# Counting the last edges in tiles as well, in place of gathering their rows (graph network, two layers)

## The chip, the cores and the metric

One NeuronCore of a Trainium2 chip runs the kernel. The metric is the device time of one execution in microseconds. The engines are named as in the profile: PE (TensorE, PEld its weight loads), DVE (VectorE), ACT (ScalarE), POOL (GpSimd) and SP (SyncE, which here only issues DMAs).

## The reference

A graph of 6250 nodes with 128 features has 206,250 edges, sorted by destination `dst`. Layer 0 is a linear map with batch norm and a normalized sum over edges; layer 1 sums the 128 attributes of each edge into its destination and puts the result through three linear maps.

```python
h = jnp.maximum(_layernorm(x), 0.0)
H = h @ W.T + b                       # then batch norm over the nodes
dinv = rsqrt(1.0 + segment_sum(ones, dst))
msg = H[src] * (dinv[src] * dinv[dst])[:, None]
out = segment_sum(msg, dst) + H * (dinv * dinv)[:, None]
x = x + relu(out)
h = jnp.maximum(_layernorm(x), 0.0)
agg = segment_sum(edge_attr, dst)
z = relu(concat([h, agg, u[batch]]) @ W1 + b1)
x = x + relu(z @ W2 + b2) @ W3 + b3
```

## The kernel before, in words

The kernel runs five stages, each a block with one hand-written instruction stream per engine, tied by semaphores.

1. **Opening.** Loads, layer norm, linear map, degree counts. Besides the edge rows for the attributes it loads the last 27,648 edges' `dst` and `src` (`raw_g`) and turns them into `grel` and `index`.
2. **Plan.** The scaled features H·dinv are put into `table_sb` in SBUF as two fp16 parts, high and low, and written to the DRAM tensor `scaled_h_table`. The nodes are dealt out in groups of WN = 3. A tile holds up to 128 edges of one group. `gather_sources` reads the 128 `src` entries that start at each tile's first edge (14 indirect DMAs by POOL, one per 128 tiles) and from them come `src_lo` (source modulo 128) and `key` (source block times 3, plus which of the 3 destination nodes). Groups with more than 128 edges get spare tiles.
3. **Step loop,** S = 27 steps, the bulk of the time. On PE a step `s` has
   - *build*: TS = 68 tiles; `build_tile` multiplies `lo_hot` by `key_hot` (both compared into being by DVE, eight tiles at a time, an "oct", 9 per step, the ninth with only 4 tiles), a 128x147 table of counts, into `ps_counts`. ACT copies four tiles at a time (a "quad") into `counts_sb` (`save_quad`, 17 per step).
   - *multiply*: 98 products (49 blocks x high and low) of `table_sb` with the counts of the *previous* step, 204 columns each (68 tiles x 3 nodes), dealt out between the builds by `PART`.
   - *attributes*: `sum_attr`, 60 matmuls (120 PE passes) with `attr_hot` in three batches, whose sums are put into place by a `place` matmul with a `place_hot` and added by DVE (`add`).
   - *rows*: the last 27,648 edges are not counted but gathered: POOL issues 8 indirect DMAs per step that fetch rows of `scaled_h_table` into `gathered`, with four buffers (`rows_used` frees them, so that they run up to two steps ahead); `sum_rows` sums them with `half_hot`, 16 matmuls at q = 13 and q = 30, plus a fourth place, copy and add.
   - The edge attributes stream in beside all this, three loads of 1280 KB per step from SP.
   Step 13 is the step of the spare tiles; in steps 15 to 23 DVE adds 8 spare groups each (`add_spares`, L1436). The first three steps stand apart, the others are a PE loop of two steps per round. DVE, ACT and POOL are written out in full.
4. **Last product** of the loop (98 products with nothing to build).
5. **MLP.** Layer norm, three linear maps, output.

The order inside a step is set by hand: PE by the tile number `q` (`SUM_AT`, `ROWS_AT`, the `if q ==` lines), DVE by the oct number `b`, ACT by the quad number `k`. POOL issues its gathers in one queue, each pair of a step waiting for `rows_used`.

Of the kernel before, what the change touches and what calls it, by code (L numbers as in the profile page):

```python
# [8 lines left out]
F16 = mybir.dt.float16  # L9
# [9 lines left out]
GR = 2  # L19
GG = GR * P  # L20
# [7 lines left out]
KINDS = R + 1  # L28
WN = 3
TS = 68  # L30
# [6 lines left out]
def gnn_kernel(nc, x, src, dst, edge_attr, w_gcn, b_gcn, gamma, beta, u, w1, b1, w2, b2, w3, b3, out):  # L37
# [12 lines left out]
    KC = KINDS * S  # L50
# [8 lines left out]
    EDGES = E - GB * GG  # L59
    assert D == P and FULL == R * GB - 2 and E % GE and GB <= P and KEYS <= 256  # L60
    assert FB == NB - 1 == (CHUNKS - 1) * BC and AW >= NB * P and CC % DB == 2 * S % DB == 0 and N < NOWHERE / 2
    assert MC <= GC and MAIN * WN <= N and 0 < EDGES <= E - P and DEGS >= NB
# [5 lines left out]
    table = nc.dram_tensor("scaled_h_table", (NB * P, 2 * P), F16, kind="Internal").ap()  # L68
    src_elements = src.rearrange("(e a) -> e a", a=1)
    attr_last = edge_attr[E - GE:E, :].rearrange("(p t) f -> p (t f)", t=GT)  # L70
    x_full = x[0:FB * P, :].rearrange("(b p) f -> p b f", p=P)
    table_blocks = table.rearrange("(b p) f -> p b f", p=P)
    out_full = out[0:FB * P, :].rearrange("(b p) f -> p b f", p=P)

    with ExitStack() as ctx:
# [17 lines left out]

        dinv = sb("dinv", [P, NB])
# [3 lines left out]
        grel = sb("grel", [P, GR, GB], I16)  # L98
# [3 lines left out]
        index = sb("index", [P, GB, GR], I32)  # L102
        slot_node = sb("slot_node", [P, KINDS, S])
        slot_now = sb("slot_now", [P, KINDS, S])
        chunk_start = sb("chunk_start", [1, S, KINDS])
        starts = sb("starts", [1, S, KINDS])
        starts_int = sb("starts_int", [1, S, KINDS], I32)
# [216 lines left out]
        with ExitStack() as scope:  # L324
            raw_d = sb("raw_d", [GB, R, GE], I32, scope)
            raw_g = sb("raw_g", [GB, 2, GG], I32, scope)
            edge_f, grow, drow = (sb(n, [GB, R, GE], scope=scope) for n in ("edge_f", "grow", "drow"))
            gather_f, gather_row, src_row = (sb(n, [GB, GG], scope=scope) for n in ("gather_f", "gather_row", "src_row"))
# [3 lines left out]
            minus_lim = sb("minus_lim", [GB, KINDS], scope=scope)  # L332
# [9 lines left out]
            group_span = sb("group_span", [GB, KINDS], scope=scope)  # L342
            lim = sb("lim", [GB, 2 * KINDS + 1], scope=scope)
# [3 lines left out]
            by_slot = sb("by_slot", [GB, KINDS, CG, W], scope=scope)  # L347
# [5 lines left out]
            start_all = sb("start_all", [P, KINDS, S], scope=scope)  # L353
# [5 lines left out]
            low_rows = ps_rows_t[0:1, 0:BC, :].rearrange("a b f -> a (b f)")[:, 0:KINDS * GB]  # L359
            high_rows = ps_rows_t[0:1, BC:2 * BC, :].rearrange("a b f -> a (b f)")[:, 0:KINDS * GB]  # L360
# [5 lines left out]
            (eps_ok, counting, dst_in, gather_dst_in, src_in, w_in, zeroed, ident_ok, consts, pen_ok, src_ok, tiles_ok,  # L366
# [20 lines left out]
            with nc.Block() as block:  # L387
# [233 lines left out]
                def _(act):  # L621
# [25 lines left out]
                    for c in range(CHUNKS + 1):  # L647
# [12 lines left out]
                        if c in TURN_AT:  # L660
                            save_turn(2 * R + TURN_AT.index(c))
# [4 lines left out]
                def _(pe):  # L666
                    def turn_rows(k):
                        if 2 <= k < 2 * R:
                            pe.wait_ge(turn_read, k - 1)
                        elif k > 2 * R:  # L670
                            pe.wait_ge(turn_read, k)
# [1208 lines left out]
```

## Time and profile before

| | |
|---|---|
| median of 3 runs | 872.0 us (870.55 to 873.07) |
| profiled execution, its own time | 876.41 us |
| its span | 874.7 us |
| granted PE clock, mean | 0.93 of full speed |
| busy over the span | PE 727.7, DVE 589.4, ACT 416.2, POOL 320.2 us |
| step loop, first half_hot to last product | 138.7 to 793.1 us |

Busy times of engines overlap, so they don't add up to the span. The profiled execution is one execution. Differences worked out from its trace are applied to the median.

### The profile page before, as it was taken

Reading aid. Unit: us, or ns where it says so; the run is one execution under the profiler, and the core shown is the slowest. Engines: PE = TensorE matmul, PEld = TensorE weight load, DVE = VectorE, ACT = ScalarE, POOL = GpSimd, SP = SyncE. Lnnn points to the kernel's source line nnn. Section 1 sums busy time; section 2 is a strip of 40 time slices with the busy share of each in tenths; the row PEclk is TensorE's granted clock in tenths of the full one; section 3 lists DMA queues with packets and bytes.
Section 4 is the critical chain, followed back from the end, with each engine's and each line's share of the span. In section 5 each row is a group of like instructions: output and inputs, shape, how many; then the busy total and the mean of one; then the engine's idle time right before and its main releaser. Section 6 shows DMA issues by size and latency. Waiting matters only on the chain. (4 is left out here: it accounts for less than half of the span.)

```text
span 874.7 us, 23162 instructions
## 1 busy us (share of the span) xinstructions
PE 727.7 (83%) x9280; PEld 579.9 (66%) x9280; DVE 589.4 (67%) x1328; ACT 416.2 (48%) x810; POOL 320.2 (37%) x318
## 2 busy tenths in 40 slices
PE   1987765399898898998889888989988888998796
PEld 0756653277777776777777667777766677887464
DVE  6997955357666666776666567767776666753854
ACT  1442553344444545455445444444544454553693
POOL 3403825543334333333333444332333333003523
PEclk9986575599999999999999999999999999999899
DMA  6101732456665556655556556555655555533013
GB/s 173 25 1 38 256 97 92 120 191 205 205 197 181 172 199 202 201 184 177 184 202 204 174 175 204 185 167 188 201 181 161 201 196 175 187 94 84 0 46 103
DMA packets 78377, 136.20 MB, mean 156 GB/s; under 512 B 6706, under 2 KB 32844, under 8 KB 78328
## 3 DMA queue, kind: packets, MB, share of 16 engines
q1 hardware_dynamic: 70904, 120.50, 42.6%
q0 software_dynamic: 7424, 15.12, 5.6%
q8 instruction: 21, 0.34, 0.2%
q14 instruction: 28, 0.23, 0.1%
HBM read 129.19 MB, written 6.41 MB: 155 GB/s over the span
## 5 line engine op out<-in xcount | busy, mean ns | idle before, releaser
L1316 ACT CAST counts_sb<-ps_counts 128x588 f16<-128x588 f32 x459 | 295.1, 651 | 337.3 <-PE ps_counts L1493 239.7
L1493 PE MATMUL ps_counts<-key_hot,lo_hot 128*128 128x147 bf16 x1836 | 368.8, 237 | 77.6 <-ACT counts_sb L1316 49.6
L1501 PE MATMUL ps_product<-counts_sb,table_sb 128*128 128x204 f16 x2646 | 403.3, 252 | 1.5 <-issue 1.3
L1304 POOL DMA_INDIRECT gathered<-scaled_h_table,index x216 | 238.1, 1102 | 382.0 <-PE ps_sums L1531 306.4
L1493 PEld LDWEIGHTS ps_counts<-key_hot,lo_hot 128*128 128x128 bf16 x1836 | 181.1, 101 | 146.1 <-issue 70.7
L1359 DVE TENSOR_TENSOR lo_hot<-src_lo,iota_key 128x1024 bf16<-128x1024 f16 (+1 forms) x243 | 160.7, 661 | 171.4 <-PE ps_counts L1493 147.5
L1501 PEld LDWEIGHTS ps_product<-counts_sb,table_sb 128*128 128x128 f16 x2646 | 236.2, 98 | 5.3 <-issue 4.1
L1364 DVE TENSOR_TENSOR key_hot<-key,iota_key 128x1176 bf16<-128x1176 f16 (+1 forms) x243 | 177.7, 731 | 0.0
L1516 PE MATMUL ps_sums<-attr,attr_hot 128*32 128x128 f32 x3240 | 130.7, 285 | 0.0
L1516 PEld LDWEIGHTS ps_sums<-attr,attr_hot 128*32 128x32 f32 x3240 | 85.4, 112 | 27.9 <-issue 19.2
L1375 DVE TENSOR_TENSOR attr_hot<-rel,iota_w 128x640 f32<-128x640 int16 x81 | 66.6, 823 | 29.1 <-remote 21.4
L1540 PE MATMUL ps_product<-place_hot,sums_sb 128*128 128x96 f32 x216 | 44.0, 286 | 0.0
L1540 PEld LDWEIGHTS ps_product<-place_hot,sums_sb 128*128 128x128 f32 x216 | 33.8, 197 | 1.8
L1419 DVE TENSOR_TENSOR acc<-acc,ps_product 128x96 f32 x108 | 26.9, 249 | 4.3 <-PE ps_product L1540 4.1
L1667 POOL TENSOR_TENSOR x_ring<-attr,b_rows 128x512 f32<-128x512 f32 (+1 forms) x13 | 15.7, 1211 | 30.7 <-DVE y_ring L1743 30.4
L1392 DVE TENSOR_SCALAR place_hot<-iota_c,slot_now 128x96 f32<-128x96 f32 x108 | 26.3, 265 | 0.0
L1531 PE MATMUL ps_sums<-gathered,half_hot 128*32 128x128 f16 x432 | 19.2, 223 | 5.4 <-issue 3.9
L1759 ACT ACTIVATE relu_ring<-ps_t,dinv 128x128 f32<-128x128 f32 x49 | 14.0, 370 | 20.4 <-PE ps_t L1807 20.0
L1653 POOL MEMSET attr<- 128x128 f32 x1 | 0.2, 205 | 59.8 <-POOLq L1277 59.8
L1326 ACT COPY sums_sb<-ps_sums 128x128 f32<-128x128 f32 x81 | 22.0, 272 | 0.0
L985 ACT ACTIVATE table_sb<-ps_rows,dinv 128x128 f16<-128x128 f32 x49 | 14.0, 381 | 15.0 <-PE ps_rows L908 14.0
L1775 ACT ACTIVATE h_ring<-attr,shift,rstd 128x128 f32<-128x128 f32 x49 | 20.1, 486 | 0.8 <-DVE shift L1701 0.8
(291 smaller groups left out, 667.6 us busy)
## 6 DMA issues: line engine op xcount, KB each, us to landing
attr<-in_edge_attr_dram SPq DMA_DIRECT2D x80, 1280.0 KB
gathered<-scaled_h_table,index POOLq DMA_INDIRECT x216
acc<-in_x_dram SPq DMA_DIRECT2D x4, 768.0 KB, 8.5
scaled_h_table<-table_sb SPq DMA_DIRECT2D x12, 256.0 KB
attr<-in_x_dram SPq DMA_DIRECT2D x12, 256.0 KB, 5.1
out_dram<-y_ring SPq DMA_DIRECT2D x12, 256.0 KB, 2.4
attr<-in_edge_attr_dram SPq DMA_DIRECT2D x2, 320.0 KB, 3.2
attr<-in_edge_attr_dram SPq DMA_DIRECT2D x1, 640.0 KB
```

The costliest lines, as they stand in the source:

```text
L1304: pool.indirect_dma_start(gathered[:, n % GATHERS, g, :], None, table, bass.IndirectOffsetOnAxis(ap=index[:, s * CG + g, t:t + 1], axis=0) ...
L1316: act.copy(counts_sb[s % 2][:].rearrange("p h (n t) -> p h n t", n=WN) [:, :, :, k * QUAD:(k + 1) * QUAD], ps_counts[n % 2][:, :, 0:KEYS]. ...
L1326: act.copy(sums_sb[:, 1, :], ps_sums[:, 1, 0:P]).then_inc(sums_saved, 1)
L1359: v.tensor_tensor(lo_hot[:, n % 2, 0:pairs], src_lo[:, tiles].rearrange("p (b c) -> p b c", c=2).unsqueeze(2) .to_broadcast(whole), iota_l ...
L1364: v.tensor_tensor(key_hot[:, n % 2, 0:pairs], key[:, tiles].rearrange("p (b c) -> p b c", c=2).unsqueeze(2) .to_broadcast(whole), iota_key ...
L1375: v.tensor_tensor(attr_hot[:, a % 2], rel[:, r, :, s * CG:(s + 1) * CG].unsqueeze(3) .to_broadcast(whole), iota_w[:].unsqueeze(1).unsqueez ...
L1392: v.tensor_scalar(place_hot[:, n % 2, :], iota_c[:], slot_now[:, kind, s:s + 1], None, ALU.is_equal).then_inc(place_hots, 1)
L1419: v.tensor_tensor(win, win, new, ALU.add).then_inc(added, 1)
L1493: ins = pe.matmul(ps_counts[(odd + quad) % 2][:, c, 0:KEYS], lo_hot[:, held, pair, :, q % 2], key_hot[:, held, pair, :, q % 2], start=True ...
L1501: ins = pe.matmul(ps_product[side][:, 0:SLOTS], table_sb[:, h, low, :], counts_sb[side][:, h, :], start=(part == 0), stop=(part == 2 * NB ...
L1516: ins = pe.matmul(ps_sums[g * W:(g + 1) * W, 1, 0:P], attr_hot[:, held, t, g, :], attr[:, j * CG + g, t * P:(t + 1) * P], start=(t == 0), ...
L1540: pe.matmul(ps_product[side][:, WIN + window * WC:WIN + (window + 1) * WC], sums_sb[:, which, :], place_hot[:, parity, :], start=True, sto ...
```

## The change

The last edges are counted in tiles like all others. TS goes from 68 to 80 tiles per step, so 26 x 80 tiles of 3 nodes cover 6240 of the 6250 nodes, and the rest fall to the spare tiles. The gathering of rows goes, with everything that served it: the `raw_g` loads, `grel`, `index`, their two turns on PE and ACT, the fourth of each KINDS table, the table in DRAM and its 13 writes, the 216 gather DMAs, `half_hot`, `sum_rows`, `save_rows`, one of the four places and adds per step. Each step's products get 240 columns in place of 204, and the octs are all full (10 per step), the quads 20. A tile now may begin within 128 edges of the end of `src`, so the source reads go to `src_padded`, a DRAM copy with 128 more entries, copied by SP in the opening; POOL waits for it ahead of its first source gather. There are 17 source gathers in place of 14, and a fifth batch of keys. The place hots are made by POOL, which has nothing else to do in the loop, and no longer by DVE.

```diff
-TS = 68
+TS = 80
...
+                    sp.dma_start(src_padded[0:E].rearrange("(a f) -> a f", f=SRC_ROW),
+                                 src.rearrange("(a f) -> a f", f=SRC_ROW)).then_inc(src_copied, 16)
...
-                    for c in range(CHUNKS):
-                        n = width(c)
-                        sp.wait_ge(low_ready, c + 1)
-                        sp.dma_start(table_blocks[:, c * BC:c * BC + n, :],
-                                     table_sb[:, c * BC:c * BC + n, :, :].rearrange("p b a f -> p b (a f)"))\
-                          .then_inc(table_out, 16)
...
-        OCTS = -(-TS // OCT)
+        OCTS = TS // OCT
...
-        SUM_AT = {q: (j, tiles) for j, places in enumerate(((5, 13), (26, 34), (47, 56)))
+        SUM_AT = {q: (j, tiles) for j, places in enumerate(((6, 15), (32, 41), (58, 67)))
                   for q, tiles in zip(places, (range(0, 3), range(3, GT)))}
-        ROWS_AT = {13: 0, 30: 1}
...
-                            pool.wait_ge(table_out, 16 * CHUNKS)
-                            for s in range(S):
-                                for t in range(GR):
-                                    n = s * GR + t
-                                    if n >= GATHERS:
-                                        pool.wait_ge(rows_used, n - GATHERS + 1)
-                                    for g in range(CG):
-                                        pool.indirect_dma_start(
-                                            gathered[:, n % GATHERS, g, :], None, table,
-                                            bass.IndirectOffsetOnAxis(ap=index[:, s * CG + g, t:t + 1], axis=0),
-                                        ).then_inc(gather_in[n % GATHERS], 16)
+                            for n in range(PLACES):
+                                s, kind = divmod(n, R)
+                                if n >= 2:
+                                    pool.wait_ge(placed, n - 1)
+                                pool.tensor_scalar(place_hot[:, n % 2, :], iota_c[:], slot_now[:, kind, s:s + 1], None,
+                                                   ALU.is_equal).then_inc(place_hots, 1)
...
-                                    if q in ROWS_AT:
-                                        sum_rows(s, odd, loads, ROWS_AT[q], first)
-                                    if q == 6 and not first:
+                                    if q == 7 and not first:
                                         pe.wait_ge(sums_saved, s * R)
-                                        place(s * 4 - 2, 0, 1, side, 0)
-                                    if q == 16 and not first:
-                                        pe.wait_ge(rows_saved, s)
-                                        place(s * 4 - 1, 1, 0, side, 1)
-                                    if q == 24:
+                                        place(s * 3 - 1, (odd + 1) % 2, side, 0)
+                                    if q == 28:
                                         pe.wait_ge(sums_saved, s * R + 1)
-                                        place(s * 4, 0, 1, side, 2, first)
-                                    if q == 42:
+                                        place(s * 3, odd, side, 1, first)
+                                    if q == 52:
                                         pe.wait_ge(sums_saved, s * R + 2)
-                                        place(s * 4 + 1, 1, 1, side, 0)
+                                        place(s * 3 + 1, (odd + 1) % 2, side, 0)
```

What moves on PE in the step loop, at tile q = 13 of a step before, where the second part of the first attribute batch and the first half of the gathered rows stand (`L1493` is a build, `L1501` a product, `L1516` the attributes, `L1531` the rows, `L1540` a place):

```order
L1501 MATMUL ps_product<-counts_sb,table_sb 128x204 x2
L1516 MATMUL ps_sums<-attr,attr_hot 32x128 x8
L1531 MATMUL ps_sums<-gathered,half_hot 32x128 x8
L1493 MATMUL ps_counts<-key_hot,lo_hot 128x147
L1501 MATMUL ps_product<-counts_sb,table_sb 128x204
```

and at the same part of a step after (`L1397` is the build, `L1405` the product, `L1420` the attributes):

```order
L1405 MATMUL ps_product<-counts_sb,table_sb 128x240
L1420 MATMUL ps_sums<-attr,attr_hot 32x128 x8
L1397 MATMUL ps_counts<-key_hot,lo_hot 128x147
L1405 MATMUL ps_product<-counts_sb,table_sb 128x240
L1397 MATMUL ps_counts<-key_hot,lo_hot 128x147
L1405 MATMUL ps_product<-counts_sb,table_sb 128x240 x2
```

The rows are gone, each product is 36 columns wider, and fewer products stand between two builds (98 dealt over 80 tiles).

DVE at the turn from one step to the next, before (`L1359` and `L1364` make an oct, `L1375` is `attr_hot`, `L1392` the place hots, `L1384` `half_hot`, `L1419` an add):

```order
L1419 TENSOR_TENSOR acc<-acc,ps_product 128x96
L1359 TENSOR_TENSOR lo_hot<-src_lo,iota_key 128x512
L1364 TENSOR_TENSOR key_hot<-key,iota_key 128x588
L1359 TENSOR_TENSOR lo_hot<-src_lo,iota_key 128x1024
L1364 TENSOR_TENSOR key_hot<-key,iota_key 128x1176
L1392 TENSOR_SCALAR place_hot<-iota_c,slot_now 128x96 x2
L1384 TENSOR_TENSOR half_hot<-grel,iota_w 128x256
L1359 TENSOR_TENSOR lo_hot<-src_lo,iota_key 128x1024
```

and after, from the last add of a step on (`L1296` and `L1301` make an oct, `L1340` is an add, `L1312` the `attr_hot`):

```order
L1340 TENSOR_TENSOR acc<-acc,ps_product 128x96
L1296 TENSOR_TENSOR lo_hot<-src_lo,iota_key 128x1024
L1301 TENSOR_TENSOR key_hot<-key,iota_key 128x1176
L1296 TENSOR_TENSOR lo_hot<-src_lo,iota_key 128x1024
L1301 TENSOR_TENSOR key_hot<-key,iota_key 128x1176
L1296 TENSOR_TENSOR lo_hot<-src_lo,iota_key 128x1024
L1301 TENSOR_TENSOR key_hot<-key,iota_key 128x1176
L1312 TENSOR_TENSOR attr_hot<-rel,iota_w 128x640
```

The half oct at a step's end is a full one, and the three small compares behind the step's first oct are gone from DVE. POOL's whole part in the loop was

```order
L1295 UNCONDITIONAL_BRANCH
L1304 DMA gathered<-scaled_h_table,index 128x256 x216
L1277 UNCONDITIONAL_BRANCH
L1243 REGISTER_ALU
L1243 COMPARE_AND_BRANCH
```

and is now

```order
L1246 UNCONDITIONAL_BRANCH
L1252 TENSOR_SCALAR place_hot<-iota_c,slot_now 128x96 x81
L1228 UNCONDITIONAL_BRANCH
L1194 REGISTER_ALU
L1194 COMPARE_AND_BRANCH
```

so that it issues no DMA there at all.

## Rows read from the trace of the kernel before

**Rows 1.** Windows: us; busy (x) PE, PEld, DVE, ACT, POOL; PEclk; DMA share; GB/s.

```profile
138.73:173.94 35.21, 18.13 (x207) 11.95 (x206) 15.20 (x30) 10.98 (x21) 24.42 (x23) 0.60 0.41 123
173.94:743.40 569.46, 505.88 (x7437) 409.46 (x7436) 390.24 (x813) 278.14 (x505) 212.50 (x192) 0.98 0.57 189
502.33:719.98 217.65, 189.72 (x2793) 154.09 (x2791) 151.99 (x348) 104.32 (x189) 80.96 (x72) 0.98 0.56 185
743.40:763.79 20.39, 19.91 (x313) 16.65 (x311) 15.85 (x33) 11.67 (x21) 0.00 (x0) 1.00 0.58 200
763.79:784.00 20.21, 20.21 (x318) 17.18 (x315) 13.78 (x29) 11.67 (x21) 0.00 (x0) 1.00 0.17 56
```

**Rows 2.** The half_hot of each step on DVE (one tile's instructions).

```profile
L1384 DVE TENSOR_TENSOR half_hot<-grel,iota_w x27: 417/419/423, 138.7 to 763.8; 128x256 f16<-128x256 int16 x27
```

**Rows 3.** Timeline of two steps around their gathers: start us, length us, idle before in brackets.

```profile
395.30 1.20 ACT L1316 CAST counts_sb<-ps_counts 128x588 f16<-128x588 f32 x2 [3.12 <-remote]
...
421.15 0.82 DVE L1375 TENSOR_TENSOR attr_hot<-rel,iota_w 128x640 f32<-128x640 int16 x1 [1.97 <-remote]
421.19 0.65 ACT L1316 CAST counts_sb<-ps_counts 128x588 f16<-128x588 f32 x1 [2.73 <-PE ps_counts L1493]
...
421.97 0.24 PE L1493 MATMUL ps_counts<-key_hot,lo_hot 128*128 128x147 bf16 x1 [1.84 <-ACT counts_sb L1316]
```

**Rows 4.** Timeline of PE in step 25: builds, products, rows, a place.

```profile
745.43 0.38 PE L1540 MATMUL ps_product<-place_hot,sums_sb 128*128 128x96 f32 x2
745.65 0.23 PE L1493 MATMUL ps_counts<-key_hot,lo_hot 128*128 128x147 bf16 x1
745.72 0.25 PE L1501 MATMUL ps_product<-counts_sb,table_sb 128*128 128x204 f16 x1
745.81 0.23 PE L1493 MATMUL ps_counts<-key_hot,lo_hot 128*128 128x147 bf16 x1
...
747.58 0.29 PE L1531 MATMUL ps_sums<-gathered,half_hot 128*32 128x128 f16 x8
747.81 0.24 PE L1493 MATMUL ps_counts<-key_hot,lo_hot 128*128 128x147 bf16 x1
...
763.57 0.24 PE L1493 MATMUL ps_counts<-key_hot,lo_hot 128*128 128x147 bf16 x1 [0.48 <-DVE key_hot L1364]
```

**Rows 5.** Timeline of step 0: the long waits.

```profile
163.60 1.38 ACT L1316 CAST counts_sb<-ps_counts 128x588 f16<-128x588 f32 x2 [5.70 <-remote]
...
172.23 1.20 ACT L1316 CAST counts_sb<-ps_counts 128x588 f16<-128x588 f32 x2 [7.25 <-remote]
```

**Rows 6.** Timeline of ACT: copies of quads in the plain part of a step.

```profile
387.21 1.45 ACT L1316 CAST counts_sb<-ps_counts 128x588 f16<-128x588 f32 x2 [1.03 <-PE ps_counts L1493]
```

**Rows 7.** Timeline of the opening: POOL compares, a DVE operation under a POOL memset, edge work.

```profile
28.28 0.53 POOL L462 TENSOR_SCALAR ident_part<-ident 128x128 f16<-128x128 f32 x1
...
68.71 3.66 DVE L183 TENSOR_SCALAR unscale<-ident,size 128x128 f32<-128x128 f32 x1
...
66.90 5.39 POOL L482 MEMSET acc<- 128x6346 f32 x1 [34.60 <-DVE h_ring L556]
...
17.15 0.28 DVE L506 CAST gather_f<-raw_g 108x256 f32<-108x256 int32 x1
...
18.46 0.16 DVE L510 TENSOR_REDUCE lim<-tile_min 108x3 f32<-108x15 f32 x1
```

**Rows 8.** Groups by line, the plan's costs: us busy, mean ns.

```profile
L1064 DVE TENSOR_TENSOR passed<-count_row,sizes 128x1792 f16<-128x1792 f16 x3 | 3.6, 1195 | 0.0
```

**Rows 9.** Timeline of the plan's end: source gathers, the stall, the last two key batches.

```profile
114.83 1.13 POOL L225 DMA_INDIRECT spare_raw<-in_src_dram,spare_int  x1 [0.30 <-issue]
115.90 0.59 ACT L992 COPY acc<-ps_self 128x512 f32<-128x512 f32 x1 [4.28 <-remote]
...
130.89 0.59 ACT L1004 CAST key<-ps_keys 128x512 f16<-128x512 f32 x1 [1.38 <-PE ps_keys L934]
...
133.60 0.35 ACT L1004 CAST key<-ps_keys 128x232 f16<-128x232 f32 x1 [1.34 <-PE ps_keys L934]
```

More of the change, by code:

```diff
@@ L442, in _ @@
                     pool.wait_ge(lims, 1)
-                    for r in range(KINDS):
+                    for r in range(R):
                         whole = [GB, CG, W]
@@ L687, in _ @@
                     pe.wait_ge(lims, 1)
-                    for k in range(2 * KINDS + 1):
-                        if k < KINDS:
+                    for k in range(2 * R + 1):
+                        if k < R:
                             row = low_rows[:, k * GB:(k + 1) * GB]
-                        elif k < 2 * KINDS:
-                            row = high_rows[:, (k - KINDS) * GB:(k - KINDS + 1) * GB]
+                        elif k < 2 * R:
+                            row = high_rows[:, (k - R) * GB:(k - R + 1) * GB]
                         else:
@@ L706, in find_slots @@
                         pe.wait_ge(consts, CONSTS)
-                        for r in range(KINDS):
+                        for r in range(R):
                             of_slot = by_slot[:, r].rearrange("g c n -> g (c n)")
@@ L1192, in _ @@
                         def _(sp):
-                            for s in (summed, rows_used, last_in, x_loaded, *attr_in):
+                            for s in (summed, last_in, x_loaded, *attr_in):
                                 sp.sem_clear(s)
@@ L1347, in _ @@
                         def _(v):
-                            regs = [[v.alloc_register(f"start{k}_{j}") for j in range(KINDS)] for k in range(2)]
+                            regs = [[v.alloc_register(f"start{k}_{j}") for j in range(R)] for k in range(2)]
                             base_regs = [v.alloc_register(f"base{j}") for j in range(SPARE_ADDS)]
@@ L1520, in sum_attr, with place @@
                                     ins.then_inc(summed, 1)
-                            def sum_rows(s, odd, loads, t, first):
-                                if t == 0:
-                                    pe.wait_ge(rows_hots, s + 1)
-                                    if not first:
-                                        pe.wait_ge(rows_saved, s)
-                                held = odd * GR + t
-                                pe.wait_ge(gather_in[held], loads)
-                                for part in range(2):
-                                    for g in range(CG):
-                                        ins = pe.matmul(ps_sums[g * W:(g + 1) * W, 0, 0:P], half_hot[:, t, g, :],
-                                                        gathered[:, held, g, part * P:(part + 1) * P],
-                                                        start=(t == 0 and part == 0), stop=(t == GR - 1 and part == 1))
-                                ins.then_inc(rows_used, 1)
-                            def place(n, parity, which, side, window, first=False):
+                            def place(n, parity, side, window, first=False):
                                 pe.wait_ge(place_hots, n + 1)
```

249 lines of the change are left out of this document (81 added, 168 removed).

## The prediction

> **What bounds the kernel now.** I first cut the loop into steps, at the half_hot that DVE makes once in each [rows 2], and asked for the busy time in windows between them [rows 1]. Steps 1 to 24 take 569.46 us, 23.73 each, with PE busy 505.88 of it, DVE 390.24, ACT 278.14. PE is the engine that sets the pace, but it is idle 63.6 us, 2.6 per step. The next two windows show what that idle time is. POOL's gathers run up to two steps ahead, so that the last two steps, 25 and 26, have none (POOL 0.00). They take 20.39 and 20.21 us, with PE busy for 19.91 and 20.21. Step 25 has its other work whole, and its DMA traffic is even a little higher (200 GB/s against 189), so bandwidth isn't what the other steps lack.
>
> The timeline shows what a step with gathers suffers. Once in each, while POOL is issuing, all engines that wait for PE stand still together: at 421.15 and 421.19 DVE and ACT come out of waits of 1.97 and 2.73 us at the same moment, and PE, having run ahead, then waits 1.84 us for ACT; a step earlier ACT waited 3.12 us [rows 3]. The profile calls the releaser "remote", that is, it found none. In step 0, where POOL issues 23 of them in one series [rows 1], the same waits are 5.70 and 7.25 us [rows 5], and in the plan, at the end of the series of source gathers, 4.28 us [rows 9]. I don't know the mechanism. What I rely on is that the waits stand where POOL issues indirect DMAs, and that two steps without them have none.
>
> **The change, term by term** (as a difference; the profiled execution took 876.41 us, its span 874.7, the median is 872.0, and I take the same difference for each).
>
> *Stall removed.* If all 24 steps ran like step 25 they would save 24 x (23.73 - 20.39) = 80.1 us. Not all of the excess is the gathers'. The nine steps with spare adds average 24.18 (217.65 / 9), the other fifteen (569.46 - 217.65) / 15 = 23.45; the 0.73 of difference, 6.6 us in sum, is DVE's and stays. Some 1.2 us I leave for the first product step, in which PE's clock is still rising. That leaves **-72.3 us**.
>
> *PE's added work per step.* In the clean step a product takes 0.09 us from start to start, a build 0.07, a group of rows 0.23 (747.58 to 747.81), a place 0.22 [rows 4]. A product of 240 columns scales to 0.087 x 240/204, which is 0.015 more (0.087 is an estimate over several pairs of these rows); 98 of them +1.50. Twelve builds at 0.073: +0.88. Three more quad boundaries, about +0.1. Two groups of rows: -0.46, one place: -0.22. At the start of the step PE waits 0.48 for DVE, because the half oct covers only four tiles while DVE makes the next; with full octs I take off half of it, -0.24. Sum +1.56, so a clean step is 20.39 + 1.6 = 22.0. Bounds: 21.6 if the wait goes whole and a boundary costs nothing; 22.9 if another pacer comes in (below). Over steps 1 to 26: 26 x 1.6 = **+41.6 us**.
>
> *Who hides the rest.* DVE makes 10 octs for 8.5; even if its whole 15.85 us grew with them it would be busy 18.6 of 22.0 us, and it loses half_hot, the place hots and one add: still hidden. ACT goes from 17 to 20 quads of 0.65: 11.67 becomes at most 13.6. Two quads in a row take ACT 1.45 and one takes 0.65, so they follow one another at 0.80 [rows 3, 6]. PE's four builds and their share of products take about 0.80 both before (4 x 0.073 + 5.8 x 0.087) and after (4 x 0.073 + 4.9 x 0.102), so ACT is no closer to the path than it was, but it has no slack. The edge loads have 22 us for what now passes in 20.4.
>
> *Step 0* takes 35.21 us at a clock of 0.60. Its two long waits are 12.95 us; waits of PE for gathered rows are another 1.4 (an estimate, between nothing and the 7.25 of its longest wait). What is left, 20.9 us for 8.5 octs, is 2.3 per oct without its first; 1.5 octs more cost 3.4. Sum **-10.9 us**. If these waits had another cause it would be +3.4.
>
> *Last product.* 98 x 0.015 = **+1.5 us**.
>
> *Plan.* The three compares (3.6 us together [rows 8]) grow by 17/14: +0.8. The spare compares, for which no row stands here, grow by 80/68; bounded by the same 3.6 us group and nothing, I take +0.8. At the end, batches of keys follow one another at 2.7 us (130.89 to 133.60) [rows 9], each waiting on the one before: the fourth batch has four columns in place of two and there is a fifth of one column: +2.4, between +1.6 and +5.4. Three more source gathers are three more POOL instructions of some 1.13 us [rows 9], behind which only the last batches' data wait; 0, or up to +4 if the stall of 4.28 us there grows with the series. Writing the table to DRAM goes and may shorten that stall; the two I let cancel. Sum **+4.0 us**.
>
> *Opening.* DVE is rid of the four operations between 17.15 and 18.46 [rows 7], in a run without idle time: -1.3, and of smaller tables: **-1.4 us**. The copy of `src` is issued by SP behind the loads of x, and the first to need it is the plan's first source gather, behind the whole opening (its row at 68.71 is still ahead of that) [rows 7].
>
> *Spare adds* now take ten steps, not nine: **+0.7 us**.
>
> Sum: -72.3 + 41.6 - 10.9 + 1.5 + 4.0 - 1.4 + 0.7 = -36.8. From 872.0 that gives **835 us**.
>
> **A rule that speaks against the change.** While POOL's memset of 5.39 us ran, a DVE compare-sized operation on 128x128 took 3.66 us, where POOL itself needs 0.53 for one of that size, and it ended with the memset [rows 7]: the two engines can hold each other up. The place hots put 81 POOL operations of about 0.53 us (by the compare of 128x128 [rows 7]) beside DVE's compares. The Trainium skill states it as a rule (SBUF — State Buffer, "Who interferes with whom"): a DVE instruction with two SBUF inputs contends with a GpSimd instruction that reads SBUF, and whoever comes second waits in full. By that rule DVE could lose 3 x 0.53 = 1.6 us per step. The trace agrees on a blocking as such; how much of it reaches PE it can't show. From the rows alone: DVE has at least 3.4 us idle per step (22.0 less 18.6), in which 1.6 us fit, so I price it at 0, with the whole 1.6 as the worst.
>
> **The rivals.**
> - *Another pacer, 11 in 100.* The stall goes, but the step comes out at 22.8, because ACT's quads (no slack, above) or DVE's late octs hold PE: 26 x 0.8 = +21, and half of step 0's long waits stay, +6: 862. For it: the 0.80 on both sides. Against: step 25 shows PE 19.91 busy of 20.39 with the same ratio.
> - *Everything a little better, 13 in 100.* A clean step is 21.6 (-10), the spare adds hide in it now that DVE isn't thrown back by the stall (-7), the plan's stall is gone (-3): 815.
> - *Slower, 5 in 100.* The place hots on POOL hold up DVE, and through the octs PE. They sit between the octs, three per step. To eat the whole gain the step must lose 36.8 / 26 = 1.4 us more, 0.47 us per place hot, of the 0.53 that one lasts: nearly each would have to be passed on in full. With the 1.6 of the worst case and the other terms at their high bounds the time is about 885. Against it stands DVE's idle time.
> - *The change doesn't do what it says, 1 in 100.* If there were more spare tiles than 80 the whole loop would run twice, some 600 us more. Groups of three nodes have 99 edges on average, so few pass 128.
> - The forecast as it stands: 70 in 100, its own range 822 to 850.
>
> **How the numbers follow.** The likeliest case gives 835. The range reaches down to the better case and up towards the other pacer: 815 to 858. A difference of 0.3% (2.6 us) is about what a measurement of this kernel can tell from none. Faster gets the forecast, the better case and the other pacer: 0.94; slower 0.05; the same 0.01, since nothing but a chance sum of mishaps ends there.
>
> **What would show it.** Steps of 21.6 to 22.3 us in the windows, all alike but for the spare steps, with PE at least 97% busy and the granted clock at 1.00 throughout (0.98 over the gathered steps [rows 1]). No wait of ACT of 2 us or more with the releaser "remote" inside steps. Step 0 near 24 us. DVE 16 to 18 us per step; POOL about 1.6 us. Products 15 ns longer. The plan's end some 4 us later relative to its start. Wrong I would be if the waits of 2 to 3 us are still there without the gathers (then they belong to code loading or the like, and the time is near 905), if PE shows short waits for ACT at each quad, or if DVE's compares grow longer beside POOL.

## The result, and the profile after

Beside each other on one chip the kernel before takes 872.35 us and the changed one **811.63 us** (ratio 0.929, 95% interval 0.926 to 0.931): 60.7 us less, where I had forecast 37. The direction is right, the size is not, and the time lies 3 us below my range. The experiments then added what this pair doesn't show: in three of the five later sets of runs the same kernel before took 781 to 783 us, and in the one of them in which the changed kernel ran too, it was the slower, at 803.9.

First the page of the changed kernel: busy time, then PE, POOL and PE's clock in 40 slices.

```profile
span 807.7 us, 22520 instructions
PE 724.6 (90%) x9123; PEld 589.2 (73%) x9123; DVE 611.8 (76%) x1230; ACT 464.8 (58%) x864; POOL 203.6 (25%) x184
PE   1876565899999999999999999999999999999797
POOL 3402880222222112222211221222221121204424
PEclk9997755899999999999999999999999999999899
```

PE stays at 9 from the first product step to the end of the loop. Now both traces, cut at the same marks: start of the plan, first lo_hot of the loop (step 0), first lo_hot of step 1, first lo_hot of step 25, last product taken, end. These are the prediction's own stretches: step 0 by itself, then steps 1 to 24. Windows (columns as in [rows 1]), first of before:

```profile
83.33:136.70 53.37, 33.62 (x274) 29.97 (x274) 34.75 (x109) 25.56 (x75) 27.51 (x29) 0.63 0.51 160
136.70:172.29 35.59, 17.93 (x204) 12.02 (x204) 15.58 (x27) 9.37 (x18) 25.64 (x24) 0.60 0.39 120
172.29:741.75 569.46, 505.52 (x7429) 409.07 (x7430) 390.24 (x812) 278.29 (x506) 212.50 (x192) 0.98 0.57 188
741.75:793.12 51.37, 50.38 (x739) 43.61 (x738) 32.07 (x66) 24.80 (x45) 0.00 (x0) 1.00 0.51 160
793.12:874.70 81.58, 65.42 (x325) 43.95 (x325) 46.61 (x119) 50.77 (x126) 31.52 (x27) 0.92 0.15 42
```

and of the changed kernel, with eleven of its plain steps in the last row:

```profile
81.57:143.54 61.97, 36.75 (x289) 30.99 (x289) 37.58 (x111) 26.89 (x78) 33.34 (x33) 0.61 0.28 90
143.54:160.68 17.14, 13.32 (x199) 9.26 (x200) 16.57 (x27) 10.68 (x20) 5.30 (x4) 0.86 0.47 156
160.68:677.26 516.58, 507.88 (x7283) 423.15 (x7281) 409.43 (x727) 321.42 (x553) 103.85 (x72) 1.00 0.55 183
677.26:731.98 54.72, 54.68 (x732) 46.93 (x730) 33.05 (x55) 28.81 (x50) 7.30 (x5) 1.00 0.51 154
731.98:807.70 75.72, 63.95 (x325) 42.76 (x325) 46.65 (x119) 50.53 (x126) 31.48 (x27) 0.95 0.15 44
207.63:440.40 232.77, 232.76 (x3347) 194.79 (x3345) 182.65 (x299) 147.38 (x254) 48.36 (x34) 1.00 0.56 186
```

| piece | forecast | measured |
|---|---|---|
| start to plan | -1.4 | 81.57 - 83.33 = -1.76 |
| plan | +4.0 | 61.97 - 53.37 = +8.60 |
| step 0 | -10.9 | 17.14 - 35.59 = -18.45 |
| steps 1 to 24 | -72.3 + 24 x 1.6 + 0.7 = -33.2 | 516.58 - 569.46 = -52.88 |
| steps 25 and 26, last product | 2 x 1.6 + 1.5 = +4.7 | 54.72 - 51.37 = +3.35 |
| behind the loop | 0 | 75.72 - 81.58 = -5.86 |
| sum | -36.8 | -67.0 |

The spans differ by 67.0, the medians by 60.7: the profiled execution of before was 4.1 us above its median, that of after 1.9 below.

A plain step is 232.77 / 11 = 21.16 us with no idle time of PE, not 22.0. The steps with spares are longer. One of them on DVE (start, length), then the instruction of PE that waits for what follows the additions:

```profile
469.81 2.29 DVE L1352 TENSOR_TENSOR acc<-acc,spare_sums 128x3 f32 x8
472.01 0.69 DVE L1296 TENSOR_TENSOR lo_hot<-src_lo,iota_key 128x1024 bf16<-128x1024 f16 x1
472.62 0.76 DVE L1301 TENSOR_TENSOR key_hot<-key,iota_key 128x1176 bf16<-128x1176 f16 x1
473.44 0.24 PE L1397 MATMUL ps_counts<-key_hot,lo_hot 128*128 128x147 bf16 x1 [0.74 <-DVE key_hot L1301]
```

The eight additions take 2.29 us in a row, the oct behind them is late, and PE waits 0.74 us, once in each such step. In the plan, while POOL issues its series of source gathers, ACT still has the waits that nothing in the profile releases, the only ones left in the kernel:

```profile
117.33 0.59 ACT L954 COPY acc<-ps_self 128x512 f32<-128x512 f32 x1 [2.88 <-remote]
120.86 1.14 ACT L947 ACTIVATE table_sb<-ps_rows,dinv 128x128 f16<-128x128 f32 x4 [2.94 <-remote]
123.05 0.59 ACT L954 COPY acc<-ps_self 128x512 f32<-128x512 f32 x1 [1.05 <-remote]
```

### The profile page after: what moved, and what is told of

It is laid out like the page before. It is cut to its first block and busy times, and to the rows that moved or that the text cites. A ratio compares the mean times of both kernels' runs of the same rounds, so it can differ in the third digit from the quotient of the medians.

```text
span 807.7 us, 22520 instructions
## 1 busy us (share of the span) xinstructions
PE 724.6 (90%) x9123; PEld 589.2 (73%) x9123; DVE 611.8 (76%) x1230; ACT 464.8 (58%) x864; POOL 203.6 (25%) x184
## 5 line engine op out<-in xcount | busy, mean ns | idle before, releaser
L1262 ACT CAST counts_sb<-ps_counts 128x588 f16<-128x588 f32 x540 | 350.6, 651 | 219.8 <-PE ps_counts L1397 186.4
L1405 PE MATMUL ps_product<-counts_sb,table_sb 128*128 128x240 f16 x2646 | 442.4, 264 | 0.0
L1397 PE MATMUL ps_counts<-key_hot,lo_hot 128*128 128x147 bf16 x2160 | 410.5, 231 | 14.5 <-DVE key_hot L1301 11.7
L1296 DVE TENSOR_TENSOR lo_hot<-src_lo,iota_key 128x1024 bf16<-128x1024 f16 x270 | 186.3, 690 | 107.8 <-PE ps_counts L1397 103.4
L1397 PEld LDWEIGHTS ps_counts<-key_hot,lo_hot 128*128 128x128 bf16 x2160 | 206.7, 98 | 74.0 <-issue 43.7
L1405 PEld LDWEIGHTS ps_product<-counts_sb,table_sb 128*128 128x128 f16 x2646 | 243.5, 97 | 10.6 <-issue 0.2
L1252 POOL TENSOR_SCALAR place_hot<-iota_c,slot_now 128x96 f32<-128x96 f32 x81 | 116.6, 1439 | 471.8 <-PE ps_product L1430 449.4
L1301 DVE TENSOR_TENSOR key_hot<-key,iota_key 128x1176 bf16<-128x1176 f16 x270 | 208.8, 774 | 0.0
L1420 PE MATMUL ps_sums<-attr,attr_hot 128*32 128x128 f32 x3240 | 122.7, 279 | 0.0
L1420 PEld LDWEIGHTS ps_sums<-attr,attr_hot 128*32 128x32 f32 x3240 | 79.0, 109 | 26.0 <-issue 24.9
L1312 DVE TENSOR_TENSOR attr_hot<-rel,iota_w 128x640 f32<-128x640 int16 x81 | 66.9, 826 | 0.0
L1430 PE MATMUL ps_product<-place_hot,sums_sb 128*128 128x96 f32 x162 | 30.3, 269 | 0.0
L1052 DVE SCALAR_TENSOR_TENSOR table_sb<-ps_rows,dinv,table_sb 128x128 f16<-128x128 f32 x49 | 13.7, 340 | 9.1 <-issue 7.6
L849 POOL DMA_INDIRECT src_raw<-src_padded,begin_int x17 | 19.0, 1116 | 4.1 <-issue 4.1
```

The lines of the kernel that those rows point to most:

```text
L849: pool.indirect_dma_start(src_raw[:, k, :], None, src_elements, bass.IndirectOffsetOnAxis(ap=begin_int[:, k:k + 1], axis=0))\
L1252: pool.tensor_scalar(place_hot[:, n % 2, :], iota_c[:], slot_now[:, kind, s:s + 1], None, ALU.is_equal).then_inc(place_hots, 1)
L1262: act.copy(counts_sb[s % 2][:].rearrange("p h (n t) -> p h n t", n=WN) [:, :, :, k * QUAD:(k + 1) * QUAD], ps_counts[n % 2][:, :, 0:KEYS]. ...
L1296: v.tensor_tensor(lo_hot[:, n % 2], src_lo[:, tiles].rearrange("p (b c) -> p b c", c=2).unsqueeze(2) .to_broadcast(whole), iota_lo[:].unsq ...
L1301: v.tensor_tensor(key_hot[:, n % 2], key[:, tiles].rearrange("p (b c) -> p b c", c=2).unsqueeze(2) .to_broadcast(whole), iota_key[:].unsqu ...
L1312: v.tensor_tensor(attr_hot[:, a % 2], rel[:, r, :, s * CG:(s + 1) * CG].unsqueeze(3) .to_broadcast(whole), iota_w[:].unsqueeze(1).unsqueez ...
```

## The experiments

Behind the first pair, which is at the upper level, five sets of runs followed, each on one chip with the kernel before beside it: set 1 (782.6 us for the kernel before), set 2 (890.7), set 3 (874.4), set 4 (781.2), set 5 (782.3). Sets 2 and 4 carry the same chip number. I call 782 the lower level and 870 to 891 the upper one.

### Is it the gathers? (sets 1 and 3)

The kernel before without the gathers of its loop:

```diff
-    pool.indirect_dma_start(gathered[:, n % GATHERS, g, :], None, table, ...)   # 8 per step
+    pool.memset(gathered[:, 0], 0.0).then_inc(gather_in[0], 16)                 # once
-    pe.wait_ge(gather_in[held], loads)
+    pe.wait_ge(gather_in[0], 16)
```

> The kernel before without the 216 indirect gathers of the edge loop; one buffer of zeros stands in for all gathered rows, so the sums over gathered edges are left out of the result. All else stays: 68 tiles, the row sums on PE, the place hots on DVE, the table written to DRAM. Theory (the stalls belong to the gathers): steps 1 to 24 fall from 23.73 us to about 20.4 (20.4 + 0.73 where spares are added), no wait of ACT of 2 us or more inside a step, step 0 falls from 35.21 to 17 to 21 us, and the time from 872 to about 783 (780 to 792). Rival (the stalls have another cause, such as code or edge loads, that only happened to be absent in steps 25 and 26): steps stay at 23 us or more and the time above 855.

**Set 1: 778.9 us, ratio 0.996 (0.994 to 0.997).** The kernel before itself was at 782.6 there, so its 216 gathers cost 3.7 us. My expectation named the right time for the wrong reason: on this set there was no stall to remove.

> Again the kernel before without the 216 gathers of the edge loop and without their sums. On the first chip on which it ran, the kernel before itself was at 782.6 us and this one at 778.9. Theory (on the chips where the kernel before takes 870 to 900 us, its gathers are what freezes the engines): this kernel takes 776 to 790 us on every chip, so that on such a chip it is 90 to 110 us faster than the kernel before. Rival (those chips are slower in everything that the kernel before does, through a lower clock or slower signals): it takes 855 us or more there.

**Set 3: 783.3 us, ratio 0.897 (0.894 to 0.901).** Here the same edit is worth 91.1 us. Its windows on this set, same marks:

```profile
83.70:138.62 54.92, 32.87 (x274) 28.41 (x274) 35.74 (x110) 25.62 (x75) 30.14 (x30) 0.62 0.49 156
138.62:155.10 16.48, 12.84 (x204) 8.82 (x204) 15.21 (x28) 9.26 (x18) 0.85 (x1) 0.86 0.49 162
155.10:648.61 493.51, 476.75 (x7429) 398.70 (x7430) 388.67 (x811) 280.02 (x505) 0.00 (x0) 1.00 0.58 192
648.61:699.98 51.37, 50.37 (x739) 43.60 (x738) 32.07 (x67) 24.79 (x45) 0.00 (x0) 1.00 0.52 159
```

Against the first profile of the kernel before, steps 1 to 24 lose 569.46 - 493.51 = 76.0 us (I had 72.3), and step 0 loses 35.59 - 16.48 = 19.1, where I had 14.4. Against the kernel before's own profile in set 3 (one execution, rep_before2) it is 563.58 - 493.51 = 70.1 and, from first half_hot to second, 41.16 - 16.10 = 25.1. Steps 25 and 26 with the last product, which had no gathers anyway, stay at 51.37. Without the loop's gathers the kernel is nearly at the same time on both levels, 778.9 and 783.3 us; the rest of the difference is the plan, whose source gathers stay (50.65 us in set 1, 54.92 in set 3).

### What about a gather costs? (sets 1, 3, 4, 5)

Idle gathers added to the changed kernel; nobody reads the buffer or waits for it, and rows of x stand in for the table:

```diff
     pool.tensor_scalar(place_hot[:, n % 2, :], iota_c[:], slot_now[:, kind, s:s + 1], ...)
+    if kind < 2:                      # a_gathers4: kind < 1
+        for g in range(4):
+            pool.indirect_dma_start(gathered[:, t % 4, g, :], None, x,
+                bass.IndirectOffsetOnAxis(ap=row_index[:], axis=0)).then_inc(gather_in[t % 4], 16)
```

> The changed kernel with eight indirect gathers of 128 rows of 512 bytes per step added on POOL, four behind the place hot of the first group and four behind that of the second; they read rows of x into a buffer that nobody uses, and nothing on PE, ACT or DVE waits for them. Theory (issuing the gathers freezes the signals between the other engines): the excess of before returns though nobody waits for the data, 3.1 us per step (23.45 less 20.39), so 27 x 3.1 = 83 us and about 893 (875 to 915), with waits near 2 us of ACT and DVE once or twice in each step. Rival A (the excess was PE waiting for the rows themselves): 811 to 816, no change. Rival B (the place hots, delayed behind the gathers on POOL, are what is late): the time grows too, but with PE's waits ending on place_hot.

> The same with four added gathers per step in place of eight, all behind the place hot of the first group. If the freeze grows with the number of gathers, half of what eight cost: about +41 us, near 852. If there is one freeze per series whatever its length, each of the two series of the other kernel costs the same as this one's single series, which is again half; if there is one freeze per step, the cost is that of eight, near 893. What tells the first two apart is the length of the single wait: 1.5 us against 3.

> The changed kernel with the same 512 KB per step read from x by eight plain copies on SyncE's queue (rows of 512 bytes, 128 of them per copy), into a buffer that nobody uses. Theory (the issuing by POOL costs, not the traffic): 811 to 815, steps of 21.1 to 21.3 us. Rival (traffic into SBUF holds up the engines): as much as the eight gathers cost, near 890.

**Set 1 (lower level): 804.4, 805.0 and 802.9 us.** These are eight gathers, four gathers and eight plain copies per step, all within 1.1 us of the changed kernel's 803.9 (which is of set 5, below: it didn't run in set 1). Ten steps and more with 80 gathers, in windows:

```profile
200.04:432.88 232.84, 232.83 (x3347) 194.69 (x3345) 181.89 (x298) 147.20 (x254) 141.74 (x122) 1.00 0.64 211
```

21.17 us per step, PE never idle, at 211 GB/s. Traffic, and the issuing as such, cost nothing at this level.

> Again the changed kernel with eight idle indirect gathers of rows of x per step on POOL. On the first chip it took 804.4 us, no longer than the same bytes by plain copies (802.9). Theory: on a chip where the kernel before takes 870 to 900 us the freezes come back with the gathers, 2.5 to 3.5 us per step and 875 to 915 in all; on one where it takes 782, 802 to 807. Rival (the freezes need something else of the kernel before, such as gathers from the table that was just written, or TensorE waiting for the rows): 811 to 820 on a chip of the first kind.

> The same eight idle gathers per step, but each fetches 4 bytes for each of its 128 indices (from the padded copy of src) in place of 512. If the freeze belongs to the issuing and the number of descriptors: as a_gathers8b on the same chip. If it belongs to the bytes that they move: nothing over the changed kernel, 811 to 816 on a chip with freezes.

**Set 3 (upper level): 871.8 and 878.1 us**, where the changed kernel takes 811.6 to 813.7 (in the first pair and in set 2, at the same level). The stall is back although nobody wants the data: from one product taken to the next it is mostly 23.4 to 23.5 us (233.70 for ten in a row) against 21.15. It is 2.3 us for eight gathers, less than the 3.1 that I expected. With 4 bytes per index in place of 512 it isn't smaller, so it is not the bytes. Nor is it a late place hot (rival B): in a_gathers8b the profile ends no wait of another engine with one. A piece of that run's trace (the idle time before an instruction is in brackets):

```profile
300.35 0.24 PE L1409 MATMUL ps_counts<-key_hot,lo_hot 128*128 128x147 bf16 x1 [0.17 <-issue]
300.46 0.95 POOL L1263 DMA_INDIRECT gathered<-in_x_dram,row_index  x1 [0.30 <-issue]
...
300.97 0.23 PE L1409 MATMUL ps_counts<-key_hot,lo_hot 128*128 128x147 bf16 x1
...
301.04 0.65 ACT L1274 CAST counts_sb<-ps_counts 128x588 f16<-128x588 f32 x1 [0.82 <-PE ps_counts L1409]
301.04 0.69 DVE L1308 TENSOR_TENSOR lo_hot<-src_lo,iota_key 128x1024 bf16<-128x1024 f16 x1 [1.63 <-PE ps_counts L1409]
...
301.71 1.53 POOL L1263 DMA_INDIRECT gathered<-in_x_dram,row_index  x1 [0.31 <-issue]
...
302.50 0.26 PE L1417 MATMUL ps_product<-counts_sb,table_sb 128*128 128x240 f16 x1
302.55 0.65 ACT L1274 CAST counts_sb<-ps_counts 128x588 f16<-128x588 f32 x1 [0.85 <-PE ps_counts L1409]
303.32 0.24 PE L1409 MATMUL ps_counts<-key_hot,lo_hot 128*128 128x147 bf16 x1 [0.56 <-issue]
303.54 0.95 POOL L1263 DMA_INDIRECT gathered<-in_x_dram,row_index  x1 [0.30 <-issue]
```

PE stands for 0.56 us before the build at 303.32, which starts a new quad, and the profile names no releaser. But the kernel does: the build needs ACT's copy of the quad before the last. That quad's builds are those from 300.35 to 300.97, and its copy is the one at 302.55; PE starts 0.12 us after the copy's end. So PE isn't late. The copy is: it starts 1.58 us after the last build of its quad, where a copy that finds ACT free starts 0.27 us after it. DVE comes out of its own wait for PE's builds at 301.04, in the same moment as ACT.

The whole trace says the same. 156 of its 540 copies start more than 0.7 us after the last build of their quad, up to 2.4 us; in the changed kernel none does (0.67 at most). And of the 106 times that PE takes more than 0.35 us from the instruction ahead to the first build of a quad, 105 end within 0.15 us of the end of the copy or the key_hot that the build needs. What the gathers hold up is the hop from PE to ACT and DVE; the hop back is prompt. The Trainium skill says that PE and ACT never wait on anyone in SBUF (SBUF — State Buffer, "Who interferes with whom"). If that holds, ACT doesn't wait for a port here but for PE's signal; no run here shows which.

> Again four idle gathers per step in place of eight. Where eight cost 60 us (2.3 us per step, 23.45 against 21.15): if the freeze grows with the number of gathers, 22.3 us per step and about 843 in all; if there is one per step whatever the number, as with eight, about 872. On a chip without freezes 803 to 806.

> Eight idle gathers per step, each of 32 rows in place of 128. If the freeze grows with the descriptors: about a quarter of 60 us, 826 in all (steps of 21.7 us). If it is the instruction alone: as eight whole gathers, about 872.

> Eight idle plain copies per step (128 rows of 512 bytes each, as the gathers, at fixed addresses) issued by GpSimd in place of the gathers. If every transfer whose descriptors GpSimd writes freezes the engines: about 872. If only the indirect ones do: 811 to 820.

> Four idle gathers per step in the changed kernel, in a set of runs whose level isn't known beforehand. Where the kernel before takes 870 us or more: 843 and steps of 22.3 us if the freeze grows with the number of gathers, 872 and steps of 23.4 if there is one freeze per step whatever their number. Where the kernel before takes 782: 803 to 806 and steps of 21.15, as twice before.

**Inconclusive.** These four asked what the freeze grows with, and fell on sets at the lower level, where there is none: 803.8, 804.4, 803.7 (set 4) and 804.9 us (set 5). They only confirm that idle transfers are free there. Whether the freeze grows with the number of gathers or of descriptors, and whether plain copies issued by GpSimd cause it too, stays open.

### The two levels (sets 2, 3, 5)

> The kernel before itself, unchanged, for its profile. In the last set of runs it took 782.6 us, where it had taken 872 us beside the changed kernel. Theory (the freezes that accompany the gathers depend on the chip or its condition, not on the program): its time is one of the two levels, near 782 or near 872; where it is near 782, steps 1 to 24 last 20.4 to 21 us with the gathers running as before and no wait of ACT of 2 us or more, and step 0 lasts 17 to 21 us; where it is near 872, all is as in the first profile. Rival (the low level is a matter of single executions): both levels appear among its runs on one chip.

> The kernel before once more, for its profile on this chip. Near 782 us (a chip on which gathers disturb nothing), or between 870 and 900 (one on which they do), and nothing between.

> The changed kernel itself, unchanged. Theory: where the kernel before takes 782 us, the changed one takes 803 (800 to 806), since its steps are 21.15 us on either level and only its plan gets shorter, by the 7 to 8 us of its waits; it is then slower, at a ratio of 1.026. Where the kernel before takes 872, it is 811 and the ratio 0.93. Rival (the two kernels move together): the ratio stays near 0.93 wherever they run.

> The changed kernel itself, unchanged. Where the kernel before takes 782 us: 802 to 805, a ratio of 1.027, with steps of 21.15 us and the plan 8 to 9 us shorter than in its first profile. Where the kernel before takes 870 us or more: 810 to 815.

The kernel before took 891.4 us in set 2 and 878.4 (one run) in set 3; within a set its runs never changed level. It isn't the chip alone: sets 2 and 4 carry one chip number and stand at different levels. What sets the level stays open. **The changed kernel took 813.7 in set 2 (ratio 0.917, 0.908 to 0.926) and 803.9 in set 5 (ratio 1.028, 1.025 to 1.031).** Plan and steps of the last one:

```profile
81.82:136.53 54.71, 33.75 (x289) 29.97 (x289) 36.91 (x112) 26.62 (x78) 33.40 (x33) 0.62 0.31 102
154.09:670.65 516.56, 507.83 (x7283) 423.12 (x7281) 409.38 (x728) 321.04 (x553) 103.78 (x72) 1.00 0.55 183
```

Steps 1 to 24 are the same to 0.02 us on both levels; the plan is 61.97 - 54.71 = 7.3 us shorter at the lower one, and the waits "remote" on ACT are gone from it. So what the changed kernel keeps of the freeze sits in its source gathers.

### What the change adds (sets 2 and 4)

Products of 204 columns in the changed kernel:

```diff
-    ins = pe.matmul(ps_product[side][:, 0:SLOTS], table_sb[:, h, low, :], counts_sb[side][:, h, :], ...)
+    wide = SLOTS if part == 0 else 204
+    ins = pe.matmul(ps_product[side][:, 0:wide], table_sb[:, h, low, :], counts_sb[side][:, h, 0:wide], ...)
```

> The changed kernel with 97 of the 98 products per step 204 columns wide in place of 240 (the first keeps 240); the sums of the last twelve tiles of each step lack those parts. Nothing else changes. My forecast had 0.015 us per product for the 36 columns: steps of 21.15 - 1.46 = 19.7 us. The trace of the changed kernel, read by starts, gives 0.0133 less the gaps: 19.85 (27 steps and the last product, 36 us in all: 776 on a chip where the changed kernel takes 812). Rival (the products are held by their weight loads of 97 ns, so that narrower ones gain little): steps of 20.5 or more.

**Set 4: 786.3 us (ratio 1.007, 1.004 to 1.009).** Eleven steps:

```profile
198.79:422.39 223.60, 222.89 (x3346) 186.44 (x3345) 182.57 (x298) 147.18 (x254) 48.41 (x34) 1.00 0.59 194
```

20.33 us per step against 21.16, so the step gains 0.83 where 97 x 0.015 would be 1.46. It lies nearer to the rival's time, but the rival's reason fails. From start to start a product takes 0.087 us here and 0.102 in the changed kernel (medians, of products that another follows and of those that a build follows alike): each is 0.015 shorter, as forecast, and starts closer behind the one before than the 0.097 that its weight load lasts. What takes half of it back stands in front of builds. First the changed kernel, then a_cols204, in its piece a copy of ACT ahead:

```profile
258.87 0.26 PE L1405 MATMUL ps_product<-counts_sb,table_sb 128*128 128x240 f16 x1
258.97 0.23 PE L1397 MATMUL ps_counts<-key_hot,lo_hot 128*128 128x147 bf16 x1
```

```profile
247.44 0.65 ACT L1262 CAST counts_sb<-ps_counts 128x588 f16<-128x588 f32 x1 [0.85 <-PE ps_counts L1397]
247.80 0.25 PE L1406 MATMUL ps_product<-counts_sb,table_sb 128*128 128x204 f16 x1
247.88 0.23 PE L1397 MATMUL ps_counts<-key_hot,lo_hot 128*128 128x147 bf16 x1
247.95 0.25 PE L1406 MATMUL ps_product<-counts_sb,table_sb 128*128 128x204 f16 x1
248.22 0.24 PE L1397 MATMUL ps_counts<-key_hot,lo_hot 128*128 128x147 bf16 x1
```

From the product at 247.95 to the build at 248.22, the first of a quad, are 0.27 us, not 0.09: the build starts 0.13 after the end of ACT's copy (247.44 + 0.65). Such stops, counted as what a product followed by a build takes beyond the usual, sum to 0.86 us per step here and to 0.32 in the changed kernel. PE got faster and ran into ACT's copies; that returns 0.54 of the 1.46. PE's busy time shows little of this (222.89 of 223.60 us), since a product counts as busy for 0.25 us from its start.

> The changed kernel with its 81 place hots made by VectorE again (as before the change), between the octs, and none by GpSimd. Theory (each has slack for them, 0.2 us of VectorE three times per step against 21.15 us with some 16.6 busy, and the 1.49 us that GpSimd takes for one is not waited for): within 2 us of the changed kernel either way. Rival (on GpSimd they hold up VectorE through the memory that both read): 5 us or more faster than the changed kernel.

**Set 2: 814.0 us beside 813.7.** The place hots cost the same on either engine.

> The changed kernel with the eight additions of spare sums per step (2.29 us in a row on VectorE, behind the seventh oct) cut into two groups of four, behind the fourth and the seventh oct. Theory (the ten steps with spares are 0.9 us longer because TensorE waits 0.74 us for a late key_hot, once in each): these steps become 21.2 us like the others and the time falls by 7 to 9 us. Rival (the additions also cost elsewhere, or two groups make two waits): 0 to 3 us less.

```diff
-    if b == 6 and 0 <= s - SPARE_STEP - 2 < -(-SPARES // SPARE_ADDS):
-        add_spares(s)
+    if b in (3, 6) and 0 <= s - SPARE_STEP - 2 < -(-SPARES // SPARE_ADDS):
+        add_spares(s, (3, 6).index(b))      # four of the eight
```

**Set 2: 804.9 us, 8.8 less than the changed kernel (ratios to before 0.907 and 0.917).** Eight steps with spares:

```profile
506.12:675.42 169.30, 169.30 (x2435) 141.67 (x2433) 140.42 (x282) 107.04 (x185) 35.37 (x25) 1.00 0.56 186
```

169.30 / 8 = 21.16, a plain step, with PE never idle. At the upper level this version beats both kernels. At the lower one it wasn't run; 803.9 less 8.8 would be some 795, still behind the kernel before (an estimate).

## Why the prediction was right and wrong

**The stall belongs to the gathers: right, and now shown.** Removing them alone gives 91.1 us in set 3, and adding idle ones brings back 58 to 60. In the steps its size was right too: 70 to 76 measured, 72.3 forecast.

**"What is left, 20.9 us for 8.5 octs, is 2.3 per oct": this step failed.** I took the visible waits (12.95 and 1.4) out of step 0 and kept the rest as its cost. But the rest was slowed as well: that stretch ran at a granted clock of 0.60 [rows 1]. Without gathers step 0 runs at 0.86 and takes 16.48 us. The waits were 14.4 of the 19.1 that it loses; the same PE instructions were busy for 17.93 us before and 12.84 now, 5.1 less, about the other part. With the changed kernel's octs step 0 takes 17.14, some 0.7 more (at the lower level 17.56 against 17.25), where I had 3.4. Together 7.5 us of the miss.

**PE's added work per step, "Sum +1.56": this step failed most.** Measured from one clean step to another it is 21.15 - 20.39 = 0.76, over 26 steps some 22 us less than forecast. The columns were priced right: start to start a product takes 0.087 us before and 0.102 after. What I mis-sized are the stops of PE, "At the start of the step PE waits 0.48 for DVE [...] I take off half of it, -0.24" and "about +0.1" for the quad boundaries. From the product ahead to that build are 0.73 us (start to start), where 0.09 is usual, so the stop costs 0.64 and not 0.48, and with full octs all of it goes. With the shorter stops behind ACT's copies, PE's stops sum to 1.04 us in a clean step before and 0.32 after: -0.72, where my terms give -0.14. The twelve builds cost 0.67 rather than 0.88. Together that is the 0.8. So I added PE's work to a step that had room in it, and counted only half of the one gap that I saw.

**Spare adds: +0.7 was too little.** Without gathers eight steps have 0.62 each (21.02 against 20.39); the ninth adds only four groups, not eight, and costs nothing (20.40). They became ten full ones with 0.9 and more: +4.5 between the no-gather kernel and the changed one. I carried over the wait without asking whether a shorter slack per oct makes it longer. a_split_spares shows that it is all DVE's 2.29 us in a row.

**Plan: +4.0 in work was right**, 50.65 us without the freeze before (b_no_gathers, set 1) against 54.71 (rep_after2). The other 4.6 us are the stall at its gathers, which I had bounded at "up to +4 if the stall of 4.28 us there grows with the series" and taken at 0.

**Last product and opening: right** to 0.5 us (3.35 less two steps of 0.76 leaves 1.8 for the last product, where I had 1.5). **Behind the loop: unforeseen.** No operation changed there, yet all profiled executions of before and its variant take 79.7 to 82.3 us from the last product taken, those of the changed kernel and its variants mostly 75.7 to 76.7, some up to 81.9. What tips it stays open; it gave 4 to 6 us.

**The place hots on POOL: right that they cost nothing**, wrong in their length:

```profile
L1252 POOL TENSOR_SCALAR place_hot<-iota_c,slot_now 128x96 f32<-128x96 f32 x81 | 116.6, 1439 | 471.8 <-PE ps_product L1430 449.4
```

1.44 us in the mean, not 0.53, and 0.52 at the shortest; POOL was the one that was held up, and nobody waited for it. DVE's key_hot took 0.778 us with them (rep_after) and 0.765 without (a_place_dve, same windows).

**What no case of mine held: that the stall might not be there.** I gave "slower" 5 in 100, through DVE. At the lower level the change is slower because no stall is there to be removed: from 778.9 without gathers to 803.9 it adds 25.0 us (by the pieces of the table, from b_no_gathers to rep_after2, -1.7 + 4.1 + 0.3 + 23.1 + 3.4 - 4.2), and the gathers that it removes cost 3.7. There "slower" came true, but not in the way that I named. At the upper level the time lay only 3 us outside the range because the misses ran both ways: the plan and the spare adds cost some 8 us more than I had, the steps and step 0 far less. My argument, that steps 25 and 26 show the kernel without gathers, was sound for the trace before me, and said nothing of other chips or times.

## What to carry to other kernels

Before you rebuild a kernel to be rid of a wait whose releaser the profile can't name, time the kernel before in more than one set of runs: here the same program stood at 782 and at 872 to 891 us, and the verdict on the change has the opposite sign at either level. When a stall is taken out of a low-clock stretch, take the clock out with it: read the rest from a stretch at full clock. When you price added work on an engine, list its stops first, from start to start, with what each waits for: here half of what the wider products cost fell into a gap that closed, and a faster PE only ran into ACT's copies. And a series of short dependent operations on an engine that feeds a double buffer should be cut into pieces, shorter than the slack of one buffer; that was worth 9 us for three lines.

## What the runs showed of the hardware

- Eight indirect DMAs per step, issued by GpSimd, cost 3.7 us in all in set 1 (kernel before); in set 3 they cost some 60 (idle, in the changed kernel) and 91 us (in the kernel before), at nearly the same mean time per issue (1.15 us in a_gathers8, 1.19 in a_gathers8b). The bytes don't matter (4 or 512 per index: 878.1 and 871.8 us), nor whether anyone waits for them.
- Where they cost time, what comes late is the start of ACT and DVE after PE's builds (ACT's copy up to 2.4 us after, 0.27 when undisturbed). PE starts within 0.15 us of the copy or compare that it waited for.
- A product of 240 columns takes 0.102 us from start to start, one of 204 takes 0.087. A step of 97 such products gained only 0.83 us of the 1.46, because PE then stopped longer for ACT's copies.
- A tensor_scalar of 128x96 on GpSimd took 0.52 us at its shortest and 1.44 in the mean beside VectorE's compares.
